# Moving the weight-staging loads of a recurrent block from SyncE's DMA queue to ScalarE's

## The chip, the cores and the metric

One Trainium2 chip. The program runs on 8 cores; each core takes one of the 8 sequences (4096 tokens of 1024 channels), and the cores exchange nothing. The metric is the device time of the slowest core, in microseconds, median of several runs.

## The reference, cut to what matters

```
xn = layernorm(x)                                  # no gain
h  = layernorm(xn) * gamma + beta
u, z = split(h @ in_proj_w, 2)                     # 1024 -> 2 x 2048
u  = silu(causal_conv4(u) + conv_b)
Bm = (u @ x_proj_w)[..., 16:]                      # 16 states
delta = softplus(u @ dt_proj_w + dt_proj_b)        # 2048 x 2048
h_t = h_{t-1} * exp(delta_t * A) + (u_t * delta_t) * Bm_t ;  y_t = sum over states
s  = ((y + u * D) * silu(z)) @ out_proj_w + xn
g  = silu(tanh(((xn @ weight) @ aux_weight1) @ aux_weight2 + bias))
out = x + s * g
```

The weights come as float32 in device memory; all matrix products run in bfloat16, so every weight is converted on the chip.

## The kernel before

The program is written as a list of instructions for each engine. A small recorder (class `Em`) keeps, for every buffer key, who wrote and who read it last, and puts the semaphore waits in. Each engine runs its own list strictly in the order in which the Python code emits it, and a DMA is an entry in the list of the engine that issues it: SP (SyncE) has nothing but DMAs, ACT (ScalarE) has activations and DMAs mixed. A DMA with its waits holds back everything behind it on its engine. All DMAs are recorded at line 102 or 108, so they are told apart by the tensors they move.

There are four stages, with a fence (all engines wait for all) between them:

- A start, where constants and the whole input projection `w_in` (16 pieces of 1 MB) are brought in.
- Stage A, 8 chunks of 512 tokens. In each chunk four `x` tiles are loaded (SP, two buffers `xb`), normalized twice on DVE with small helper activations on ACT (lines 321 to 348; the first ACT one is L333), transposed by PE, and multiplied by `w_in` (PE L408, ACT evictions L417 and L422). Then ACT stores the chunk's `up_sp` (2 MB) and calls `drain_w0(5)`.
- Stage B, 8 chunks of 512 tokens. Convolution on DVE (L465 to L480) from one buffer `upv` that SP loads from `up_sp`, silu on ACT (L484), 16 broadcast stores `bmrep_sp` from ACT's queue, the product with `w_dt` (PE L514), softplus (ACT L528 and L531), stores `d_sp` and `w_sp`; `drain_w0(5)` at the end of each chunk.
- The scan over time (L590 to L634), and the last stage with the output projection and the three feed-forward products.

`drain_w0` is the routine in question. It works through a list of 72 conversion jobs: 16 of `w_in` (all before stage A), 16 of `w_dt`, 16 of `w_out`, 24 of the three feed-forward weights. 40 of them stand at the ends of the 8 chunks of stage A (16 `w_dt`, 16 `w_out`, 8 `w_f`), and 16 in stage B (5, 5, 5 and 1 at the ends of the first four chunks). A job loads a float32 piece (1 MB for `w_in` and `w_dt`, 512 KB for the others) into one of two staging buffers `wstg0/1`, ACT converts it (L277 straight into `win_sb`, L297 into `wcv0/1`), and for all but `w_in` ACT's queue stores the bfloat16 piece to a scratch tensor (`wf_dt`, `wf_out`, `wf_f`; 512 or 256 KB). All stores of one scratch tensor have one key, so each waits until the one before has landed. In the kernel before the loads are SP's, so SP can be up to two jobs ahead of ACT; what stands behind them on SP, the `x` loads of the next chunk in stage A and the `up_sp` load of the next chunk in stage B, waits until SP is through with the chunk's loads.

Of the kernel before, what the change touches and what calls it, by code (L numbers as in the profile page):

```python
# [139 lines left out]
def build_program():  # L140
# [36 lines left out]
    em = Em()  # L177

    from contextlib import ExitStack
    with ExitStack() as stack:  # L180
# [36 lines left out]
        wstg = [WB.a([128, 2048], F32) for _ in range(2)]  # L217
# [45 lines left out]
        def drain_w0(njobs):  # L263
            for _ in range(njobs):
                i = w0_state["i"]
                if i >= len(w0_jobs):
                    return
                w0_state["i"] = i + 1
                kind, k, hh, dst = w0_jobs[i]
                par = i % 2  # L270
                if kind == "win":
                    src = w_in[k * 128:(k + 1) * 128, hh * 2048:(hh + 1) * 2048]
                    em.dma("sync", wstg[par][:], src,
                           reads=[], writes=[f"wstg{par}"],
                           stream=f"wstg{par}")
                    em.emit("scalar", lambda h, k=k, hh=hh, par=par:
                            h.activation(  # L277
                                win_sb[:, k, hh * 2048:(hh + 1) * 2048],
                                wstg[par][:], AF.Copy),
                            reads=[f"wstg{par}"], writes=["win"])  # L280
                else:
                    if kind == "dt":
                        src = w_dt[k * 128:(k + 1) * 128, :]
                        ncol = 2048
                        dkey = "wfdt"
                    elif kind == "out":
                        src = w_out[k * 128:(k + 1) * 128, :]
                        ncol = 1024
                        dkey = "wfout"
                    else:  # L290
                        src = (w_f1, w_f2, w_f3)[int(kind[1])][
                            k * 128:(k + 1) * 128, :]
                        ncol = 1024
                        dkey = "wf" + kind
                    em.dma("sync", wstg[par][:, 0:ncol], src,
                           writes=[f"wstg{par}"], stream=f"wstg{par}")
                    em.emit("scalar", lambda h, p=par, n=ncol: h.activation(  # L297
                        wcv[p][:, 0:n], wstg[p][:, 0:n], AF.Copy),
                        reads=[f"wstg{par}"], writes=[f"wcv{par}"])
                    em.dma("scalar", dst[k * 128:(k + 1) * 128, :],  # L300
                           wcv[par][:, 0:ncol],
                           reads=[f"wcv{par}"], writes=[dkey],
                           stream=f"wsc{par}")

        drain_w0(16)

        WK.reset()
# [44 lines left out]
        for c in range(NC):  # L352
            t0 = c * TC
            for ti in range(4):
                par = ti % 2
# [47 lines left out]
            for jo in range(2 * NJ):  # L403
# [16 lines left out]
                else:  # L420
# [9 lines left out]
                   reads=[f"up{cp}.{j}" for j in range(NJ)],  # L430
                   writes=[f"upsp{c}"], stream=f"upsp{cp}")
            drain_w0(5)

        em.fence()
# [15 lines left out]
        for c in range(NC):  # L450
# [57 lines left out]
            for jo in range(NJ):  # L508
                bk = jo % 4
                jp = jo % 2  # L510
                def mmfn(h, jo=jo, bk=bk, uc=uc):
                    ins = None
                    for k in range(NJ):
# [32 lines left out]
                       reads=[f"wv{jp}"], writes=[f"wsp{c}.{jo}"],  # L546
                       stream=f"wsp{jp}")
            drain_w0(5)

        em.fence()  # L550
# [115 lines left out]
        for c in range(NC4):  # L666
# [25 lines left out]
            for st in range(3):  # L692
                wsb = wfs[st]
                src = (xnc, h1, h2)[st]
# [40 lines left out]
            for ti in range(4):  # L735
                par = ti % 2
# [123 lines left out]
```

How the kernel before makes its waits and increments, by code:

```python
    def run(self, eng, handle, smap):  # L105
        for waits, fn, sem, amt in self.ops[eng]:
            for s, v in waits:
                handle.wait_ge(smap[s], v)
            ins = fn(handle)
            if ins is not None:
                ins.then_inc(smap[sem], amt)
```

## Time and profile before

| | us |
|---|---|
| median of 3 runs (lowest, highest) | 8546.5 (8543.9, 8580.69) |
| the profiled execution, its own time | 8539.65 |
| its span on the slowest core (core 3) | 8538.1 |
| start up to the first product, 0 to 151 | 151 |
| stage A, 151 to 1291 (without its first normalization) | 1140 |
| stage B, 1291 to 3005 | 1714 |
| scan, 3005 to 7490 | 4485 |
| last stage, 7490 to 8538 | 1048 |
| busy over the span: PE, DVE, ACT, POOL | 2755.4, 5205.2, 1809.1, 3246.4 |

How to read it: a row of the timeline gives the start, the busy time, the engine, the line, the operation with output and input, and in brackets how long the engine was idle before it and what ended that. `ACTq` and `SPq` are the DMA-issuing instructions of ACT and SP; their time is that of issuing, not that of the transfer. "Landing" is from the issue to the last byte's semaphore.

### The profile page before, as it was taken

What the parts mean: (1) busy time and instruction counts of PE and PEld (TensorE: products, weight loads), DVE (VectorE), ACT (ScalarE), POOL (GpSimd) and SP (SyncE); (2) the same over time, 40 slices, a digit from 0 to 9 for tenths busy, and PEclk for the clock granted to TensorE, in tenths of its full rate; (3) what the DMA queues carried; (4) which work ended last, traced back from release to release, by engine and by line L of the source; (5) the groups of instructions that cost most, each with busy time, mean ns of one, the idle gap of its engine ahead of it and who ended that gap; (6) DMA issues with size and microseconds to landing.
All of it is one profiled execution on the core that took longest, in us unless ns stands there. A gap on an engine that the chain in (4) does not pass through costs nothing.

```text
span 8538.1 us, 37387 instructions; the slowest of 8 cores (8502.7 to 8538.1 us)
## 1 busy us (share of the span) xinstructions
PE 2755.4 (32%) x9728; PEld 1013.9 (12%) x9728; DVE 5205.2 (61%) x2734; ACT 1809.1 (21%) x1683; POOL 3246.4 (38%) x524
## 2 busy tenths in 40 slices
PE   3344351222344412222222222222222222247666
PEld 1122120111111100000000000000000000013233
DVE  2332422333444469898989898999999999910000
ACT  3222220111111122221222122222222222201111
POOL 0000000000000074444555443999999999900000
PEclk9667675666666655555555555555555555568888
DMA  3322124444433320000000001000000000023332
GB/s 120 123 79 93 68 79 87 76 76 83 65 65 65 57 86 15 30 15 30 15 30 15 30 15 64 20 30 15 30 22 22 27 18 30 3 79 101 109 94 83
DMA packets 368734, 461.20 MB, mean 54 GB/s; under 512 B 149904, under 2 KB 297744, under 8 KB 360208
## 3 DMA queue, kind: packets, MB, share of 16 engines
q1 hardware_dynamic: 222352, 280.51, 10.8%
q10 hardware_dynamic: 146176, 178.31, 9.8%
q8 instruction: 85, 1.39, 0.1%
q14 instruction: 121, 0.99, 0.0%
HBM read 280.48 MB, written 178.26 MB: 54 GB/s over the span
## 4 chain that ended last, share of the span: by engine, by line
DVE 38%; DMA 14%; PE 14%; issue 13%; POOL 10%; ACT 6%; ACTq 4%; SPq 1%; DVEq 1%; POOLq 0%
DVE work L603 28%; POOL work L594 9%; PE psf L408 5%; PE psf L702 4%; ACTq L102 4%; DMA work<-wf_out 4%; DMA bmrep_sp<-bsb 2%; DMA d_sp<-work 2%; PE psf L683 1%; DVE work L470 1%; DVE work L480 1%; DVE work L475 1%; ACT work L531 1%; ACT work L484 1%; DVE work L534 1%
## 5 line engine op out<-in xcount | busy, mean ns | idle before, releaser
L594 POOL TENSOR_TENSOR work<-work,wrega 128x2048 bf16<-128x2048 bf16 x512 | 3182.9, 6237 | 4289.5 <-issue 3042.5
L616 PE MATMUL psf<-work,idb 128*128 128x512 bf16 x2048 | 955.1, 620 | 3487.5 <-DVE hstt L609 1752.1
L603 DVE TENSOR_TENSOR_SCAN work<-wregb,hstt,work 128x2048 bf16<-128x2048 f32 x128 | 1038.2, 8149 | 0.0
L603 DVE TENSOR_TENSOR_SCAN work<-work 128x2048 bf16<-128x2048 f32 x128 | 972.3, 7596 | 97.2 <-ACT wregb L590 45.8
L603 DVE TENSOR_TENSOR_SCAN work<-wregb,work 128x2048 bf16<-128x2048 f32 x128 | 1023.7, 7998 | 11.7 <-issue 0.9
L590 ACT ACTIVATE work<-work,aneg 128x2048 f32<-128x2048 f32 x256 | 508.5, 1998 | 2248.3 <-DVE work L634 1270.3
L603 DVE TENSOR_TENSOR_SCAN work<-work,hstt 128x2048 bf16<-128x2048 f32 x128 | 933.5, 7332 | 46.3 <-ACT work L590 41.5
L590 ACT ACTIVATE wregb<-work,aneg 128x2048 f32<-128x2048 f32 x256 | 508.5, 1998 | 1203.2 <-DVE work L603 1189.7
L616 PEld LDWEIGHTS psf<-work,idb 128*128 128x128 bf16 x2048 | 221.7, 126 | 4219.2 <-issue 4219.2
L514 PE MATMUL psf<-work,wrega 128*128 128x512 bf16 x2048 | 515.1, 413 | 430.7 <-DVE work L522 428.0
L534 DVE TENSOR_TENSOR work<-work 128x512 f32<-128x512 f32 x128 | 88.6, 692 | 701.9 <-ACT work L531 701.9
L321 DVE TENSOR_TENSOR work<-work 128x1024 f32<-128x1024 f32 x64 | 78.1, 1220 | 668.9 <-DMA work<-x_tm 665.5
L408 PE MATMUL psf<-work,wrega 128*128 128x512 bf16 x2048 | 467.6, 393 | 0.0
L728 POOL TENSOR_TENSOR wregb<-work 128x4096 f32<-128x4096 bf16 x8 | 63.3, 7907 | 984.3 <-ACT work L723 984.3
L749 DVE TENSOR_TENSOR work<-psf,work 128x1024 f32<-128x1024 f32 x32 | 39.2, 1224 | 521.3 <-PE psf L741 510.2
L702 PE MATMUL psf<-work,wrega 128*128 128x512 bf16 x1536 | 335.5, 379 | 15.7 <-ACT work L713 15.1
L683 PE MATMUL psf<-work 128*128 128x512 bf16 x1024 | 254.1, 408 | 235.8 <-DMA work<-wf_out 229.6
L689 DVE TENSOR_TENSOR work<-psf,work 128x512 bf16<-128x512 f32 x64 | 44.3, 691 | 436.0 <-PE psf L683 436.0
L514 PEld LDWEIGHTS psf<-work,wrega 128*128 128x128 bf16 x2048 | 206.5, 104 | 738.7 <-issue 620.2
L493 PE MATMUL psf<-work,xp 128*16 128x512 bf16 x128 | 46.4, 543 | 726.0 <-ACT work L484 582.4
L713 ACT ACTIVATE work<-psf 128x512 bf16<-128x512 f32 x128 | 76.4, 597 | 822.3 <-PE psf L702 822.3
L367 PE MATMUL psb<-idb,work 128*128 128x128 bf16 x256 | 32.4, 306 | 657.1 <-DVE work L348 657.1
(60 smaller groups left out, 2474.1 us busy)
## 6 DMA issues: line engine op xcount, KB each, us to landing
work<-x_tm SPq DMA_DIRECT2D x64, 512.0 KB, 5.3
d_sp<-work ACTq DMA_DIRECT2D x128, 256.0 KB, 2.1
work<-d_sp SPq DMA_DIRECT2D x32, 1024.0 KB, 4.8
work<-wf_out SPq DMA_DIRECT2D x64, 512.0 KB, 4.3
wregb<-w_in SPq DMA_DIRECT2D x16, 1024.0 KB, 6.0
wregb<-w_dt SPq DMA_DIRECT2D x16, 1024.0 KB, 7.8
sz_sp<-work ACTq DMA_DIRECT2D x128, 128.0 KB, 1.7
up_sp<-work ACTq DMA_DIRECT2D x8, 2048.0 KB, 11.5
```

Of the source, the lines that this page charges most:

```text
L102: return self.emit(eng, lambda h: h.dma_start(out=out_ap, in_=in_ap), reads=reads, writes=writes, dma=True, stream=stream)
L408: ins = h.matmul(bankf(bk), win_sb[:, k, jo * 128:(jo + 1) * 128], xh_fm[cp][:, k, :], start=(k == 0), stop=(k == NK - 1))
L470: h.scalar_tensor_tensor(a1[:], upv[:, j, 1:1 + TC], cwt3[:, 1, j:j + 1], a0[:], ALU.mult, ALU.add),
L475: h.scalar_tensor_tensor(a0[:], upv[:, j, 2:2 + TC], cwt3[:, 2, j:j + 1], a1[:], ALU.mult, ALU.add),
L514: ins = h.matmul(bankf(bk), wdt_sb[:, k, jo * 128:(jo + 1) * 128], uc[:, k, :], start=(k == 0), stop=(k == NJ - 1))
L534: em.emit("vector", lambda h, jp=jp: h.tensor_tensor(dout[jp][:], dpre[jp][:], dl[jp][:], ALU.max), reads=[f"dpre{jp}", f"dl{jp}"], writes ...
L590: h.activation(dab[sp][:], dj[jp][:], AF.Exp, scale=aneg3[:, j, s:s + 1]),
L594: h.tensor_tensor(pbf[sp][:], wj[jp][:], brep[:, s, :], ALU.mult),
L603: h.tensor_tensor_scan(hb[hp][:], dab[sp][:], pbf[sp][:], init, ALU.mult, ALU.add),
L616: ins = h.matmul(bankf(q), idb[:], hb[hp][:, q * 512:(q + 1) * 512], start=(s == 0), stop=False)
L683: ins = h.matmul(bankf(bk, TC4), wot[wp][:, k, :], ybc[:, k, :], start=(k == 0), stop=(k == NJ - 1))
L702: ins = h.matmul(bankf(bk, TC4), wsb[:, k, jo * 128:(jo + 1) * 128], src[:, k, :], start=(k == 0), stop=(k == NK - 1))
```

## The change

Both loads in `drain_w0` are issued from ACT's list instead of SP's. Sources, sizes, buffers, semaphores and the place in the Python code are as before.

```
                 if kind == "win":
                     src = w_in[k * 128:(k + 1) * 128, hh * 2048:(hh + 1) * 2048]
-                    em.dma("sync", wstg[par][:], src,
+                    em.dma("scalar", wstg[par][:], src,
                            reads=[], writes=[f"wstg{par}"],
                            stream=f"wstg{par}")
...
-                    em.dma("sync", wstg[par][:, 0:ncol], src,
+                    em.dma("scalar", wstg[par][:, 0:ncol], src,
                            writes=[f"wstg{par}"], stream=f"wstg{par}")
```

On ACT, at the start of the program, the row before (`wregb` is the staging and conversion memory, `wrega` holds `win_sb`):

```order
L242 ACTIVATE ddg<-wregb 128x2048
L246 ACTIVATE xp<-wregb 128x256
L277 ACTIVATE wrega<-wregb 128x2048 x16
L333 ACTIVATE cells<-cells 128x1
L339 ACTIVATE cells<-cells 128x1
```

and the same place now:

```order
L242 ACTIVATE ddg<-wregb 128x2048
L246 ACTIVATE xp<-wregb 128x256
L102 DMA wregb<-w_in 128x2048
L277 ACTIVATE wrega<-wregb 128x2048
L102 DMA wregb<-w_in 128x2048
L277 ACTIVATE wrega<-wregb 128x2048
L102 DMA wregb<-w_in 128x2048
L277 ACTIVATE wrega<-wregb 128x2048
```

Each of the 16 loads now stands behind the conversion of the load before it, and not in a list of its own.

On ACT, at the end of the first chunk of stage A (a piece of the difference; `up_sp` is the chunk's 2 MB store):

```order
 L102 DMA sz_sp<-work 128x512
 L102 DMA up_sp<-work 2048x1x512
+L102 DMA wregb<-w_dt 128x2048
 L297 ACTIVATE wregb<-wregb 128x2048
 L102 DMA wf_dt<-wregb 128x2048
+L102 DMA wregb<-w_dt 128x2048
 L297 ACTIVATE wregb<-wregb 128x2048
 L102 DMA wf_dt<-wregb 128x2048
+L102 DMA wregb<-w_dt 128x2048
 L297 ACTIVATE wregb<-wregb 128x2048
 L102 DMA wf_dt<-wregb 128x2048
```

Load, conversion and store of a job now stand one behind the other on one engine; the first load stands behind the `up_sp` store.

On SP, the row before, from the last constant on:

```order
L102 DMA wregb<-xpw_t 128x256
L102 DMA wregb<-w_in 128x2048 x16
L102 DMA work<-x_tm 128x1024 x4
L102 DMA wregb<-w_dt 128x2048 x5
L102 DMA work<-x_tm 128x1024 x4
L102 DMA wregb<-w_dt 128x2048 x5
```

and now:

```order
L102 DMA wregb<-xpw_t 128x256
L102 DMA work<-x_tm 128x1024 x32
L102 DMA wrega<-wf_dt 128x2048 x16
L102 DMA work<-up_sp 128x16x512
L102 DMA work<-up_sp 128x16x515 x7
```

Nothing stands between the `x` loads any more, nor between the `up_sp` loads. The lists of PE, DVE and POOL are unchanged.

## Rows read from the trace of the kernel before

**Rows 1.** Waits of DVE: engine, line, releaser: total us, times, longest.
```profile
DVE work L321 <- DMA work<-x_tm: 665.5, 8, 90.3
```
**Rows 2.** Windows, core 3: stretch, length, busy per engine, PEclk, DMA share, GB/s.
```profile
151.00:1291.00 1140.00, 523.24 (x2503) 249.71 (x2500) 321.49 (x617) 302.00 (x508) 0.00 (x0) 0.70 0.25 87
217.00:230.00 13.00, 0.00 (x0) 0.00 (x0) 0.00 (x0) 0.28 (x2) 0.00 (x0) 0.50 0.87 279
```
**Rows 3.** Timeline of ACT, start of the program: start, busy us, [idle before].
```profile
23.01 1.91 ACT L277 ACTIVATE wrega<-wregb 128x2048 bf16<-128x2048 f32 x1 [8.02 <-DMA wregb<-w_in]
...
88.35 0.20 ACT L333 ACTIVATE cells<-cells 128x1 f32<-128x1 f32 x1 [3.04 <-DVE cells L330]
```
**Rows 4.** Chain of waits, 60 to 90: start us, length us, what.
```profile
60.01 1.92 ACT wrega L277
...
62.00 5.67 DMA wregb<-w_in
...
67.81 1.92 ACT wrega L277
```
**Rows 5.** Timeline of ACT, end of stage A's first chunk.
```profile
212.27 0.56 ACTq L102 DMA_DIRECT2D up_sp<-work  x1
...
244.73 0.20 ACT L333 ACTIVATE cells<-cells 128x1 f32<-128x1 f32 x1 [1.41 <-DVE cells L330]
```
**Rows 6.** Timeline of SP in the same stretch.
```profile
214.92 17.39 SPq L102 DMA_DIRECT2D wregb<-w_dt  x3
232.35 16.54 SPq L102 DMA_DIRECT2D work<-x_tm  x3
```
**Rows 7.** Timeline of ACT, end of the fourth chunk.
```profile
680.33 0.54 ACTq L102 DMA_DIRECT2D up_sp<-work  x1
...
704.64 0.20 ACT L333 ACTIVATE cells<-cells 128x1 f32<-128x1 f32 x1 [3.81 <-DVE cells L330]
```
**Rows 8.** Timeline of ACT, end of the fifth chunk.
```profile
826.95 0.54 ACTq L102 DMA_DIRECT2D up_sp<-work  x1
...
850.47 0.20 ACT L333 ACTIVATE cells<-cells 128x1 f32<-128x1 f32 x1 [1.88 <-DVE cells L330]
```
**Rows 9.** Timeline of DVE behind stage A's last chunk (its up_sp: 1268.46).
```profile
1290.85 0.10 DVE L455 MEMSET work<- 128x48 bf16 x1 [81.41 <-DMA wf_f<-wregb]
```
**Rows 10.** Timeline of ACT, end of stage B's first chunk.
```profile
1550.05 0.33 ACTq L102 DMA_DIRECT2D w_sp<-work  x1
1550.75 1.06 ACT L297 ACTIVATE wregb<-wregb 128x1024 bf16<-128x1024 f32 x1 [2.57 <-DVE work L541]
...
1574.39 1.28 ACT L484 ACT_TABLE_LOAD   x1 [4.33 <-DVE work L480]
```
**Rows 11.** Timeline of DVE in the same stretch.
```profile
1571.26 0.49 DVE L465 TENSOR_SCALAR work<-work,cwt 128x512 f32<-128x512 bf16 x1 [21.35 <-DMA work<-up_sp]
```
**Rows 12.** Timeline of ACT, end of stage B's fourth chunk.
```profile
2208.92 0.33 ACTq L102 DMA_DIRECT2D w_sp<-work  x1
...
2212.16 1.28 ACT L484 ACT_TABLE_LOAD   x1 [1.76 <-DVE work L480]
```
**Rows 13.** Landing times of the w_dt loads (16).
```profile
DMA to landing us min/median/max: 5.7/7.8/11.7
```
**Rows 14.** Landing times of the w_out tensor's loads (16).
```profile
DMA to landing us min/median/max: 3.7/5.3/8.4
```
**Rows 15.** DMA issues between 1409 and 1424: KB, median us to landing.
```profile
u_sp<-work ACTq DMA_DIRECT2D x1, 2048.0 KB, 7.2
```
**Rows 16.** Landing times of wf_dt stores and reloads.
```profile
DMA to landing us min/median/max: 2.6/3.2/14.6
```
**Rows 17.** ACT behind the broadcast stores: first chunk of stage B.
```profile
1474.58 1.28 ACT L528 ACT_TABLE_LOAD   x1 [65.48 <-DMA bmrep_sp<-bsb]
```
**Rows 18.** The same in the fifth chunk, whose up_sp load runs beside it.
```profile
2333.30 1.28 ACT L528 ACT_TABLE_LOAD   x1 [68.22 <-DMA bmrep_sp<-bsb]
```

**Rows 19.** DMA issues of the whole program: KB each, median us to landing.
```profile
up_sp<-work ACTq DMA_DIRECT2D x8, 2048.0 KB, 11.5
```

More of the change, by code:

```diff
@@ L272, in drain_w0 @@
                     src = w_in[k * 128:(k + 1) * 128, hh * 2048:(hh + 1) * 2048]
-                    em.dma("sync", wstg[par][:], src,
+                    em.dma("scalar", wstg[par][:], src,
                            reads=[], writes=[f"wstg{par}"],
@@ L294, in drain_w0 @@
                         dkey = "wf" + kind
-                    em.dma("sync", wstg[par][:, 0:ncol], src,
+                    em.dma("scalar", wstg[par][:, 0:ncol], src,
                            writes=[f"wstg{par}"], stream=f"wstg{par}")
```

## The prediction

> **What bounds the kernel now.** I read the windows by stage first, then the waits of DVE, then the timelines of ACT, SP and DVE at each place where `drain_w0` stands. The scan and the last stage hold no job of `drain_w0` (it has 72: 16 at the start, 40 in stage A, 16 in stage B), so only the first 3005 us can move. In stage A PE is busy 523 of 1140 us and every other engine less [rows 2]: the chunks are a serial chain (normalize, multiply, convert weights, normalize), and DVE stands idle 665.5 us, 8 times, until an `x` load lands [rows 1]. That wait is mostly the product's time, but its last part is the weight jobs: SP holds the `x` loads back behind the third to fifth weight load of the chunk [rows 6]. So the stretch from the `up_sp` store to the next chunk's first helper activation L333 is exposed from end to end, in each chunk, and what happens to this stretch is the whole question. Its lengths now: first chunk 212.27 to 244.73 = 32.5 us [rows 5]; the next two, read the same way, 31.7 each; the fourth (one 1 MB job, four of 512 KB) 24.3 [rows 7]; the fifth 23.5 [rows 8], the sixth and seventh 23.1 and 24.0; the eighth, to the fence, 1268.46 to 1290.85 = 22.4 [rows 9].
>
> **What the change takes away and adds.** On SP nothing stands before the `x` and `up_sp` loads any more; they come a chunk ahead, under the product. On ACT a load now stands behind the conversion of the job before. An ACT instruction that waits for a DMA holds all behind it (ACT idles 65 us behind its own 16 broadcast stores [rows 17]), so two loads are never in flight: load, convert, store-issue, load. The two staging buffers are worth nothing. The work beside which loads ran (SP's prefetch of two jobs under the product of stage A, and the other buffer's conversion) no longer covers them.
>
> **One job in series.** `w_in`: a conversion ends, the next load issues and lands 5.67 us later, and the conversion of 1.91 us starts; the chain of waits shows just this loop for one buffer, 60.01 to 67.81 = 7.8 us [rows 4]. For `w_dt` the conversion is followed by the store's issue and then the load's (0.5 us together), the load alone takes 5.7 (the minimum of [rows 13]), I add 0.9 because the 512 KB store is just ahead of it in the same queue, 0.1 for the wake-up, and 1.91: 9.1 us. For the 512 KB jobs: 0.5 + 3.7 (the minimum of [rows 14]) + 0.5 + 0.1 + 1.06 [rows 10] = 5.9 us. The minima, not the medians, because the medians are of loads that overlapped with others, and now each is alone.
>
> **Start.** The first load lands at about 20.8 (15.06 + 5.7) and the 16th conversion ends at 20.8 + 15 x 7.8 + 1.9 = 139.7. L333 follows at once, since DVE's first four operations of chunk 0 have run by then; it is at 88.35 now [rows 3]. That is +51.4 us. The gain of the early `x` load (3.0 us of L333's wait) is in it.
>
> **Stage A.** First load of a chunk: it stands in ACT's queue behind the 2 MB `up_sp` store. A store of that size alone lands after 7.2 us [rows 15]; the load's data follow (2.6 us per MB at the 400 GB/s or so that this store and the quiet loads reach, 1.3 for 512 KB). So from the `up_sp` issue: 1 MB lands at 9.8, converted at 11.8; 512 KB at 8.5, converted at 9.7. Four more jobs and 0.45 us to L333: three `w_dt` chunks 11.8 + 4 x 9.1 + 0.45 = 48.7; the fourth 11.8 + 4 x 5.9 + 0.45 = 35.9; the fifth to seventh 9.7 + 23.6 + 0.45 = 33.7; the eighth 9.7 + 23.6 + 2.2 for the last store's landing = 35.5. Against the lengths above: +16.2, +17.0, +17.0, +11.6, +10.2, +10.6, +9.7, +13.1, in sum +105.4. The vanished `x` wait is counted: L333 follows the last job in mine, and waited for DVE in the old one.
>
> **Stage B.** From the last `w_sp` issue to the table load ahead of L484 it is 24.3 us now [rows 10], and it is the `up_sp` load that ends it: DVE waits 21.35 us for it [rows 11]. That wait goes, since SP now loads `upv` as soon as the convolution has read it. What is late next is ACT: 0.4 + 3.9 + 0.1 + 1.06 = 5.5 for the first job, 4 x 5.9, 0.4: 29.5 us. Against 24.3, 25.1 and 24.5 in the three chunks that is +14.6. The fourth chunk has one job: 5.9 against 3.2 [rows 12], +2.7. The prefetched `up_sp` load now runs beside the broadcast stores in the first three chunks also, as it already does from the fourth on, and there ACT's wait is 68.2 instead of 65.5 [rows 17, 18]: 3 x 2.8 = +8.4. Stage B: +25.7.
>
> **Sum.** 51.4 + 105.4 + 25.7 = +182.5 us on the profiled execution's 8539.65 gives 8722; the median of the runs is 7 above that execution, so 8728 us.
>
> **A rule against the trace.** The slowest `wf_dt` store, the first behind an `up_sp` store, takes 14.6 us to land, against 2.6 for the quickest [rows 16]: it stands behind the 2 MB in its queue while SP's loads run beside. The moved loads inherit this place. The Trainium skill (DMA: Bandwidth & Descriptors, section "Issuing engines are not separate DMA queues") says that transfers issued by any engine run on the same 16 DMA engines, so that choosing another issuer saves only issue time. By that rule alone the bytes need what they needed and the time would be unchanged; the trace agrees on the shared engines, but the rule says nothing of the order in which ACT comes to its own DMAs.
>
> The same page's "Anatomy of one DMA" prices a transfer at about 2.0 us and its bytes at 436 GB/s, an estimate of 4.4 us for a 1 MB load; by it the start would cost some +31 us instead of +51. It is given for another issuing path; the shortest `w_in` landing in the chain shown here is 5.67, and the sum goes by that.
>
> **Bounds.** Low: no penalty behind a store and slightly quicker lone loads (7.6, 8.2, 5.4 us a job), no contention in stage B: start +48, stage A +85, stage B +11, so +144, 8690. High: the first `w_in` load took about 7.9 us before its conversion [rows 3], so 10 us a job: +87; a load behind a store waits for its whole 2.6 us [rows 16] and `up_sp` takes the 11.5 us that it takes now in company [rows 19]: 10.8 and 7.4 us a job, first conversion at 16.1 or 14: stage A +191; stage B +54. Sum +332, 8879.
>
> **The rivals.**
> - Series and crowding (about 8870, the high sum). Eight cores draw on the memory at once, and if lone loads stay as slow as overlapped ones, the high case holds. For it: medians of 6 to 8 us per MB. Against it: the minima, and that the mean demand falls by almost half when each core pauses to convert.
> - No change (8545). The transfers, not their order, bound the stretch: the DMA engines are busy 0.87 of the time between 217 and 230 [rows 2], and the chunk's bytes are the same. Against it: the first chunk's 4.2 MB of later loads and stores plus the 2 MB need some 25 us even at full rate, but in series each job adds about 3 us of empty latency and 1.91 us of conversion in which nothing moves; and at the start there is no store at all to share with, yet a conversion and a latency come bare 16 times.
> - Faster (about 8500). ACT's issue could run ahead of an activation that waits, so that loads stay two ahead; then freeing SP is all gain. In 7 chunks L333 no longer waits for DVE (1.4, 3.8 and 1.9 us [rows 5, 7, 8], say 2), and the two `x` loads no longer fall among the jobs (1 MB, 2.6 us): 7 x 4.6 = 32. The start gains 3 [rows 3], and three chunks of stage B the 4.3 us that ACT idles there [rows 10], 13: 48 in all. The point from which it decides is a 1 MB job at or below its present pace, about 6 us (32.5 for five, [rows 5]). Against it: ACT's 65 us of idleness behind its own issues [rows 17].
>
> **How the numbers follow.** Series as summed 0.84, crowding 0.11, no change 0.03, faster 0.02. A measurement tells about 0.5% (43 us) from no change. The first two are slower by more than that: 0.95; no change 0.03; faster 0.02. The range for 8 in 10 is 8665 to 8810: below the low sum by a little, since lone loads may be quicker than any row shows, and up into the crowded case.
>
> **What would show it.** In the changed profile: 16 conversions L277 about 7.8 us apart, and L333 first at about 140; from an `up_sp` issue in stage A to L333 about 49 us in the first chunks and 34 in the fifth; DVE's long wait at L321 gone, and one for ACT at L336 in its place; no DVE wait for `up_sp` from stage B's second chunk on, but one for ACT at L470; scan and last stage as before. Conversions 4 us apart would prove the series wrong, and jobs of 10 us the size of it.

## The result and the profile after

The changed kernel takes 8685.57 us (median of 10 runs, 8657.53 to 8761.15) against 8547.33 (10 runs, 8525.96 to 8580.69): a ratio of 1.0156, 95% interval 1.0134 to 1.0178, or about +138 us between the medians. The ratios here and below leave out executions in which the cores of one die ran at a lower granted clock and took over 1% longer than the other's. The forecast was 8728 with a range of 8665 to 8810, so the sign and the place were right and the size was a third too large. The profiled execution's slowest core is core 5, with a span of 8680.8.

Cores differ by some 40 us in one execution, so I compare stages by the median over the eight cores of each profile. The marks are the first L333, the memset L455 behind the fence, and the first exponential of the scan, L590; each column is a mark minus the one before.

| us | to L333 | stage A | stage B | scan to end | span |
|---|---|---|---|---|---|
| before | 85.2 | 1197.7 | 1741.8 | 5489.9 | 8516.2 |
| after | 102.2 | 1302.0 | 1759.8 | 5488.4 | 8655.5 |
| difference | +17.0 | +104.3 | +18.0 | -1.5 | +139.3 |
| forecast | +51.4 | +105.4 | +25.7 | 0 | +182.5 |

The start, as the timeline of ACT on core 5 of the changed kernel has it (start us, busy us, engine, line, operation, idle before); it answers to [rows 3, 4]:

```profile
22.96 1.91 ACT L277 ACTIVATE wrega<-wregb 128x2048 bf16<-128x2048 f32 x1 [7.35 <-DMA wregb<-w_in]
22.98 0.34 ACTq L102 DMA_DIRECT2D wregb<-w_in  x1
28.52 1.91 ACT L277 ACTIVATE wrega<-wregb 128x2048 bf16<-128x2048 f32 x1 [3.65 <-DMA wregb<-w_in]
28.54 0.34 ACTq L102 DMA_DIRECT2D wregb<-w_in  x1
...
101.25 1.91 ACT L277 ACTIVATE wrega<-wregb 128x2048 bf16<-128x2048 f32 x1 [3.29 <-DMA wregb<-w_in]
103.07 0.19 ACT L333 ACTIVATE cells<-cells 128x1 f32<-128x1 f32 x1
```

The next load is issued 0.02 us after the conversion in front of it has begun, not after it has ended at 24.87. Conversions are about 5.2 us apart, which is one load. The chain of waits (start, length, what) says the same with no conversion in it; in [rows 4] the conversions stood in the chain:

```profile
59.95 5.03 DMA wregb<-w_in
...
65.14 4.99 DMA wregb<-w_in
...
70.28 4.99 DMA wregb<-w_in
```

The end of stage A's first chunk on the same core, which answers to [rows 5]:

```profile
225.83 0.56 ACTq L102 DMA_DIRECT2D up_sp<-work  x1
226.41 2.24 ACTq L102 DMA_DIRECT2D wregb<-w_dt  x1
240.02 1.91 ACT L297 ACTIVATE wregb<-wregb 128x2048 bf16<-128x2048 f32 x1 [14.63 <-DMA wregb<-w_dt]
242.00 0.33 ACTq L102 DMA_DIRECT2D wf_dt<-wregb  x1
242.36 0.45 ACTq L102 DMA_DIRECT2D wregb<-w_dt  x1
249.84 1.91 ACT L297 ACTIVATE wregb<-wregb 128x2048 bf16<-128x2048 f32 x1 [7.91 <-DMA wregb<-w_dt]
...
275.93 1.91 ACT L297 ACTIVATE wregb<-wregb 128x2048 bf16<-128x2048 f32 x1 [6.55 <-DMA wregb<-w_dt]
277.97 0.33 ACTq L102 DMA_DIRECT2D wf_dt<-wregb  x1
278.40 0.20 ACT L333 ACTIVATE cells<-cells 128x1 f32<-128x1 f32 x1 [0.56 <-ACT wregb L297]
```

Here the series is real: the store waits for the conversion's end (240.02 + 1.91, issued at 242.00), the load stands behind the store, and the jobs are 8.5 to 9.8 us apart. Core 3, the core of the rows of before, shows from the `up_sp` issue to L333 49.1, 49.0, 47.9, 37.4, 33.1, 32.9 and 33.2 us, and 35.2 to the fence, against 32.5, 31.7, 31.7, 24.3, 23.5, 23.1, 24.0 and 22.4 before: +104.6.

The waits of DVE on core 5 (engine, line, releaser: total us, times, longest); the first and the last answer to [rows 1], the second to [rows 11]:

```profile
DVE cells L336 <- ACT cells L333: 806.7, 64, 109.8
...
DVE work L470 <- ACT work L484: 121.9, 119, 25.3
...
DVE work L321 <- DMA work<-x_tm: 10.9, 1, 10.9
```

The 665.5 us at L321 are down to 10.9, in the first chunk alone. The wait has moved on to L336, the first DVE operation that needs ACT, and grown (on core 3, where the 665.5 were, it is 781.0, after 28.3 before). In stage B the 21.35 us for `up_sp` have become 25 us for ACT. In both stages the transfer that was late is now early, and DVE waits longer.

### The profile page after: what moved, and what is told of

It reads as the page before. It is cut to its first block, busy times and chain, and to the rows that moved or that the text cites. A ratio compares the mean times of both kernels' runs of the same rounds, so it can differ in the third digit from the quotient of the medians.

```text
span 8680.8 us, 37320 instructions; the slowest of 8 cores (8636.7 to 8680.8 us)
## 1 busy us (share of the span) xinstructions
PE 2735.9 (32%) x9728; PEld 1011.1 (12%) x9728; DVE 5204.0 (60%) x2734; ACT 1810.0 (21%) x1683; POOL 3245.8 (37%) x524
## 4 chain that ended last, share of the span: by engine, by line
DVE 37%; DMA 16%; PE 13%; issue 13%; POOL 10%; ACT 6%; ACTq 4%; SPq 1%; DVEq 1%; POOLq 0%
DVE work L603 27%; POOL work L594 9%; PE psf L408 6%; PE psf L702 4%; DMA work<-wf_out 3%; ACTq L102 3%; DMA bmrep_sp<-bsb 3%; DMA d_sp<-work 2%; DMA wregb<-w_dt 1%; DVE work L480 1%; DVE work L470 1%; DVE work L475 1%; ACT work L531 1%; ACT work L484 1%; DMA wregb<-w_f 1%
## 5 line engine op out<-in xcount | busy, mean ns | idle before, releaser
L590 ACT ACTIVATE work<-work,aneg 128x2048 f32<-128x2048 f32 x256 | 508.7, 1999 | 2246.0 <-DVE work L634 1268.8
L590 ACT ACTIVATE wregb<-work,aneg 128x2048 f32<-128x2048 f32 x256 | 508.7, 1999 | 1202.5 <-DVE work L603 1189.0
L336 DVE SCALAR_TENSOR_TENSOR cells<-cells 128x1 f32<-128x1 f32 x64 | 10.2, 159 | 806.7 <-ACT cells L333 806.7
L702 PE MATMUL psf<-work,wrega 128*128 128x512 bf16 x1536 | 335.5, 379 | 15.7 <-ACT work L713 15.1
```

Source lines behind the costliest of these rows:

```text
L590: h.activation(dab[sp][:], dj[jp][:], AF.Exp, scale=aneg3[:, j, s:s + 1]),
L702: ins = h.matmul(bankf(bk, TC4), wsb[:, k, jo * 128:(jo + 1) * 128], src[:, k, :], start=(k == 0), stop=(k == NK - 1))
```

## The experiments

Theory 1 was formed from the timeline above: a load issue on ACT is not held by the conversion that is still running in front of it, since it needs nothing of it; what holds it is an instruction in between that does need it, the store. Theory 2 is the prediction's: load, conversion, load strictly in series. Each expectation below says what its own theories 1 and 2 are. The stages of all runs are medians over the eight cores of each profile, in us. The column "0.61" is steadier than the ratio: over all executions it takes the dies whose four cores had a median granted clock of 0.61 or more, and gives their median span less that of such dies of the kernel before, run beside it (2 to 14 dies a run, 12 to 32 of before; no interval). The changed kernel's own such dies take 8648.3.

| | to L333 | stage A | stage B | scan to end | ratio to before, 95% interval | 0.61 |
|---|---|---|---|---|---|---|
| only w_in | 102.8 | 1226.4 | 1742.9 | 5487.6 | 1.0039 (1.0000 to 1.0078) | +14 |
| only the rest | 85.2 | 1297.4 | 1762.5 | 5482.8 | 1.0160 (1.0093 to 1.0227) | +121 |
| one w_in buffer | 130.8 | 1321.1 | 1759.8 | 5494.5 | 1.0246 (1.0189 to 1.0303) | +167 |
| stores on SP | 102.7 | 1276.7 | 1742.5 | 5489.4 | 1.0070 (1.0030 to 1.0110) | +63 |
| two ahead on ACT | 85.2 | 1175.7 | 1719.5 | 5490.3 | 0.9946 (0.9908 to 0.9984) | -50 |
| loads on GpSimd | 87.6 | 1218.4 | 1732.2 | 5492.1 | 0.9984 (0.9950 to 1.0018) | -10 |
| x first on SP | 86.9 | 1183.2 | 1729.0 | 5492.2 | 0.9951 (0.9922 to 0.9981) | -26 |
| spread, GpSimd | 88.7 | 1043.4 | 1703.0 | 5497.1 | 0.9786 (0.9733 to 0.9838) | -188 |
| spread, ACT | 82.8 | 1043.9 | 1708.3 | 5490.2 | 0.9773 (0.9720 to 0.9826) | -191 |

**Only the loads of w_in moved.**

```
# kernel before, the "win" branch alone
-                    em.dma("sync", wstg[par][:], src,
+                    em.dma("scalar", wstg[par][:], src,
```

> Only the 16 loads of w_in are issued from ACT, the other 56 stay on SP. Theory 1 (a load issue on ACT does not wait for the conversion in front of it, since it needs nothing of it; only the landing of the load itself is exposed): conversions L277 are about 5.2 us apart, the first L333 comes at about 103 us instead of 86, and the time is 15 us above the kernel before, about 8562. Theory 2 (load, conversion, load strictly in series, as I predicted): conversions 7.8 apart, L333 at 140, +51, about 8600.

Measured: 8609.29 us (10 runs, against 8583.02 of before beside it), ratio 1.0039. Conversions 5.2 us apart, first L333 at 103.6 on core 5. The start is theory 1's to within a microsecond. The total, expected at +15, is blurred by the granted clock: stage A, which has no edit here, takes 1195.8 us on its best core and 1226.4 in the median, so the evidence is the first column and the +14 of the dies at 0.61.

**Only the other 56 loads moved.**

```
# kernel before, the other branch alone
-                    em.dma("sync", wstg[par][:, 0:ncol], src,
+                    em.dma("scalar", wstg[par][:, 0:ncol], src,
```

> Only the other 56 loads are issued from ACT, those of w_in stay on SP. Both theories: the ends of stage A's chunks take 49, 49, 48, 37, 33, 33, 33 us from the up_sp issue to L333 as with the whole change, stage B's three about 26.6, and the time is 110 to 125 us above the kernel before, about 8665; with the run of the w_in loads alone it should add up to the whole change's +138. If a large part of the whole change's loss lay in a slower PE and not in the jobs, this run would lie under +100.

Measured: 8698.64 us, ratio 1.0160; stage A +99.7 and stage B +20.7 over before, the start unchanged. With the 17.6 us that the start of the run above takes longer this adds up to the whole change's +138, and the loss lies in the jobs. (The dies at 0.61 add up to +135. The two ratios add up to 1.0199, more than 1.0156, but within their intervals.) Core 5's chunk ends take 49.3, 49.2, 49.3, 37.5, 33.6, 33.5 and 37.1 us.

**One staging buffer for w_in.**

```
# changed kernel
-                par = i % 2
+                par = 0 if kind == "win" else i % 2
```

> The whole change, and the w_in jobs use one staging buffer instead of two, so that each load has to wait for the conversion before it. Theory 1: conversions L277 go from 5.2 to about 7.1 us apart (5.1 + 1.9 + 0.1), the first L333 to about 132 us, the time 27 to 30 us above the changed kernel. Theory 2 (the loads are already in series and the start is short for another reason, quick lone loads): nothing changes, 5.2 apart and L333 at 103.

Measured: L333 at 130.8 instead of 102.2, +28.6; time 8778.65, ratio 1.0246. The timeline of ACT on core 5:

```profile
31.20 1.91 ACT L277 ACTIVATE wrega<-wregb 128x2048 bf16<-128x2048 f32 x1 [6.17 <-DMA wregb<-w_in]
33.18 0.33 ACTq L102 DMA_DIRECT2D wregb<-w_in  x1
38.35 1.91 ACT L277 ACTIVATE wrega<-wregb 128x2048 bf16<-128x2048 f32 x1 [5.24 <-DMA wregb<-w_in]
```

Now the load is issued at 33.18, when the conversion has ended at 33.11. The one difference is the dependence through the buffer, so it is the dependence and not the place in the list that put the conversion into the loop. This is the series that I had predicted for the change, and it takes about 7.1 us a job. The total moved more than the start, +93 against the changed kernel's median. On one die of the profile the clocks are 0.594 to 0.597, and stage A, which the edit doesn't touch, is 19 us longer in the median. The dies at 0.61 take 8679.2 against the changed kernel's 8648.3, +31, which is the start's, where 27 to 30 were expected.

**The stores moved to SP.**

```
# changed kernel; besides, SP's next two x loads and next up_sp load are put ahead of the jobs
-                    em.dma("scalar", dst[k * 128:(k + 1) * 128, :],
+                    em.dma("sync", dst[k * 128:(k + 1) * 128, :],
```

> The whole change, and the stores of the converted weights are issued from SP instead of ACT; so that they don't hold back SP's other loads, the next chunk's first two x loads and the next up_sp load of stage B are put ahead of the jobs on SP. ACT's list holds only loads and conversions. Theory 1 (it is the store, which must wait for the conversion, that keeps the next load back): 1 MB conversions L297 come 5.8 us apart instead of 8.4 and 512 KB ones about 4.1 instead of 5.4; up_sp to L333 about 38, 38, 37, 31, 28, 28, 28 us; the time is about 75 us under the changed kernel, 8610. Theory 2 (strict series): conversions 7.7 and 4.9 apart, about 25 us under it.

Measured: 8633.92 us, ratio 1.0070. That is 52 below the changed kernel's median, but the kernel before that was run beside it took 8583.02 and not 8547.33; by the ratios, 1.0156 less 1.0070, it is 74, and the dies at 0.61 say 73, where 75 were expected. Core 5, first chunk:

```profile
253.06 1.91 ACT L297 ACTIVATE wregb<-wregb 128x2048 bf16<-128x2048 f32 x1 [3.50 <-DMA wregb<-w_dt]
253.13 0.34 ACTq L102 DMA_DIRECT2D wregb<-w_dt  x1
258.43 1.91 ACT L297 ACTIVATE wregb<-wregb 128x2048 bf16<-128x2048 f32 x1 [3.45 <-DMA wregb<-w_dt]
258.50 0.33 ACTq L102 DMA_DIRECT2D wregb<-w_dt  x1
```

Without the store between them the `w_dt` load too starts beside the conversion, and the jobs are mostly 5.4 us apart instead of 8.5 to 9.8. The chunk ends are 37.7, 40.2, 38.8, 30.6, 27.7, 28.3 and 28.0 us, as theory 1 had them. In sum these seven are 54 us shorter than the changed kernel's on core 5; the stage's median gained only 25 in a profile with clocks of 0.598 to 0.608.

**All loads on ACT, two jobs ahead.** Two loads stand before the first job, and one behind each job.

```
# changed kernel; load_w0() issues the next load of the list into the buffer just freed
+        load_w0()
+        load_w0()
...
                     em.dma("scalar", dst[k * 128:(k + 1) * 128, :], ...
+                load_w0()
```

> All loads on ACT as in the changed kernel, but written two jobs ahead: behind each conversion (and its store) stands the load for the job after the next, into the buffer just freed, and at a chunk's end the next chunk's first two jobs are already loaded. Theory 1 (what costs is the place of the load behind the job before it in an in-order list, not the queue it is on): the cost goes and the freed SP remains: L333 at about 83 us, up_sp to L333 about 30 us in the first three chunks and 20 to 22 from the fourth on, stage B's three ends below 20, the time about 8515, under the kernel before. Theory 2 (ACT's queue as such is the worse place, its loads lie behind the 2 MB store and cost it issue time): the ends stay above 40 and 28 us and the time above 8600.

Measured: 8533.27 us (9 runs, 8482.19 to 8620.85), ratio 0.9946; the median span of its profile is 8468.2, 48 below the kernel before's. On core 5 the first chunk's end takes 28.7 us and the fifth's 20.2:

```profile
205.24 0.55 ACTq L102 DMA_DIRECT2D up_sp<-work  x1
205.89 1.91 ACT L306 ACTIVATE wregb<-wregb 128x2048 bf16<-128x2048 f32 x1 [1.09 <-issue]
207.88 0.33 ACTq L102 DMA_DIRECT2D wf_dt<-wregb  x1
...
218.35 0.33 ACTq L102 DMA_DIRECT2D wf_dt<-wregb  x1
...
233.92 0.20 ACT L343 ACTIVATE cells<-cells 128x1 f32<-128x1 f32 x1 [1.04 <-issue]
```

The queue is the changed kernel's; only where the loads stand in ACT's list differs, and the loss of 138 us is a gain of 50 on the dies at 0.61. Stage B's first three ends, expected below 20, take 13.8 to 14.4. Theory 2 of this run (ACT's queue is itself the worse place) falls.

**The loads on GpSimd.**

```
# kernel before, in both branches
-                    em.dma("sync", ...
+                    em.dma("gpsimd", ...
```

> The kernel before with the two loads of drain_w0 issued from GpSimd, which does nothing else up to the scan. No load stands behind a conversion in a list, and none holds back SP. Theory 1: L333 at about 83 us, the ends of stage A's chunks about 30 and 21 us, stage B's 20, the time about 8510. If freeing SP gained nothing (a rival for why the change lost: that the freed loads only compete), it would be the kernel before, 8545.

Measured: 8550.37 us, ratio 0.9984 with 1 inside the interval: no gain to be told, where 35 us were expected; the dies at 0.61 gain 10, where they spread over 32 us. The start is 2.4 us later than before, and stage B 9.6 shorter. Stage A is 1186.6 on the best core, 8 below that of before, but 1218.4 in the median. The expectation that failed is that of the chunk ends. They were to take about 30 and 21 us; over the eight cores their medians are 33.7, 34.0, 32.9, 24.3, 23.8, 23.2, 21.5 and 23.3. A core's eight ends sum to 216.0 us in the median, against 217.2 in the kernel before and 195.1 in the run two ahead on ACT. So theory 1's words for this run, that nothing is held back once no load stands behind a conversion, are too simple. Core 5, first chunk, shows the wait that stayed:

```profile
212.08 0.33 ACTq L102 DMA_DIRECT2D wf_dt<-wregb  x1
...
228.72 0.33 ACTq L102 DMA_DIRECT2D wf_dt<-wregb  x1
229.15 1.91 ACT L297 ACTIVATE wregb<-wregb 128x2048 bf16<-128x2048 f32 x1 [14.73 <-DMA wf_dt<-wregb]
```

ACT waits for the first store, which was issued behind the 2 MB `up_sp` store, and two loads of GpSimd's queue run beside it. The kernel before has the same wait at the same place (core 3, in the stretch of [rows 5]), so its chunk ends are not bounded by loads alone:

```profile
230.00 1.91 ACT L297 ACTIVATE wregb<-wregb 128x2048 bf16<-128x2048 f32 x1 [12.72 <-DMA wf_dt<-wregb]
```

From the first to the second store of the first three chunks it takes 14.5, 14.9 and 15.7 us here (medians over the cores), 15.7, 14.5 and 13.9 before, and 11.3, 9.9 and 9.6 in the run two ahead on ACT. The rest of stage A's median, some 20 us, goes with this profile's mean clocks of 0.601 to 0.609; whether they had to do with the edit I can't say.

**The loads on SP, but x and up_sp first.**

```
# kernel before; the two x loads of chunk c + 1 are emitted here, and in stage B its up_sp load
+            if c + 1 < NC:
+                for ti in range(2):
+                    em.dma("sync", xb[ti][:], x_tm[...next rows...], ...)
             drain_w0(5)
```

> The kernel before, loads on SP, but SP issues the next chunk's first two x loads and the next up_sp load of stage B ahead of the jobs' loads. It gives the gain of freed SP alone, without any loss on ACT: L333 follows the last conversion by 0.5 us instead of 1.4 to 3.8, the ends of stage A's chunks about 2 us shorter than before, those of stage B about 20 instead of 24.5, less 3 us each for the up_sp load beside the broadcast stores; the time 20 to 30 us below the kernel before, about 8520. The changed kernel had this gain in it, so its gross loss is about 160.

Measured: 8519.4 us, ratio 0.9951; stage A -14.5, stage B -12.8. This is what SP's freedom is worth by itself, 27 us (26 on the dies at 0.61), and it is in the changed kernel's net: with it the gross loss is about 165. The first store of its first chunk stands against two `w_dt` loads of SP's queue, and the next store, which waits until it has landed, comes 16.1 us later (core 5, 212.90 and 228.97):

```profile
212.90 0.36 ACTq L102 DMA_DIRECT2D wf_dt<-wregb  x1
...
228.97 0.33 ACTq L102 DMA_DIRECT2D wf_dt<-wregb  x1
```

In the run with everything on ACT, two jobs ahead, the same stretch takes 10.5 us (207.88 to 218.35). There a single load stands behind the store, in the same queue. Over the cores the medians of the first three chunks are 16.1, 15.2 and 15.0 against 11.3, 9.9 and 9.6. That this makes that version the better by 7.5 us in stage A is read from the traces; no run separates the queue from the number of loads beside the store.

**The jobs spread through the chunks**, with the loads on GpSimd and then on ACT two ahead.

```
# at the end of the body of stage A's product loop, and so in stage B's loop over jo
-            drain_w0(5)
+                if jo % 6 == 5:        # stage B: if jo % 3 == 2
+                    drain_w0(1)
```

> Loads from GpSimd, and the five jobs of a chunk are no longer at its end but spread through it: one behind every sixth eviction of stage A's product, one behind every third iteration of stage B's. The conversions of 1.9 us fit between evictions 1.7 us apart with four banks in hand. If the whole cost of the jobs is that they stand exposed at the chunk ends, L333 follows the up_sp issue within 2 us, stage A loses about 200 us and stage B about 60: 8285. If the transfers or ACT slow the product down as much as they free, the time stays at 8500.

> The jobs spread through the chunks as in the run with GpSimd's loads, but the loads issued from ACT two jobs ahead. Theory 1 (place in the list decides, the queue does not): the same as with GpSimd's loads or a little better, first L333 at 84 to 86, stage A about 1042 us, stage B about 1700, and a time near 8330 on undisturbed cores, 2.5% below the kernel before. Theory 2 (ACT's queue is itself a handicap): stage A 20 us or more longer than with GpSimd's loads.

Measured: 8399.74 us, ratio 0.9786, and 8409.00 us, ratio 0.9773 (before beside it 8592.47). Stage A 1043.4 and 1043.9, stage B 1703.0 and 1708.3. The first was expected at 8285, which took the whole of the exposed ends for gain; 154 of the 200 us in stage A came, and 39 of 60 in stage B. ACT of the second, core 0, in the product of the first chunk:

```profile
158.28 0.60 ACT L427 ACTIVATE work<-psf 128x512 bf16<-128x512 f32 x1 [1.13 <-PE psf L418]
158.77 1.90 ACT L306 ACTIVATE wregb<-wregb 128x2048 bf16<-128x2048 f32 x1
160.75 0.34 ACTq L102 DMA_DIRECT2D wf_dt<-wregb  x1
161.11 0.46 ACTq L102 DMA_DIRECT2D wregb<-w_dt  x1
161.67 1.09 ACT L427 ACTIVATE work<-psf 128x512 bf16<-128x512 f32 x2 [1.00 <-PE psf L418]
...
189.69 0.60 ACT L432 ACTIVATE work<-psf 128x512 bf16<-128x512 f32 x1 [4.16 <-DMA sz_sp<-work]
...
203.68 0.60 ACT L432 ACTIVATE work<-psf 128x512 bf16<-128x512 f32 x1 [4.42 <-DMA sz_sp<-work]
```

In the first half the conversion fits between evictions. In the second half ACT waits up to 4.4 us for a 128 KB `sz_sp` store, which now lands among the weight transfers, since the eviction writes into one of only two small buffers. That some of the missing 46 us lie there is read from the trace, not tested. The two queues give the same stage A to 0.5 us, and the same total to 3 us on the dies at 0.61: with the jobs spread and the load well ahead, the issuing engine does not matter. With the jobs at the chunk ends the two runs that load two ahead differ, -10 us from GpSimd against -50 from ACT; which part of that is the queue, and which the moment at which the loads go out, is open. The rule of the Trainium skill that the prediction weighed (DMA: Bandwidth & Descriptors, "Issuing engines are not separate DMA queues") agrees with the spread runs. It says nothing of where in its engine's list a load stands.

## Why the prediction was right or wrong

**The forecast as a whole.** The sign, the stages and the size within the range came true, in part by luck. The measured 8686 lies 4 us under the prediction's own low sum of 8690; it is inside the range because the lower edge was set below that sum. What happened, some jobs in series and others not, was none of the rivals. The signs that the prediction named for its mechanism, conversions 7.8 us apart and L333 at about 140, did not appear at the start.

**Exposed ends, and the engine that sets them: right.** All of the loss lies ahead of the scan (-1.5 us behind it), in the 72 jobs. The freed `x` and `up_sp` loads did come early, and DVE's waits went where the prediction sent them, to L336 and L470.

**One job in series: wrong for w_in, right for the jobs with a store.** The step that failed is "a conversion ends, the next load issues", 7.8 us a job and +51.4 for the start; measured 5.2 and +17.0. I took the loop of [rows 4], in which a load waits for the conversion of its own buffer, for the loop of the changed kernel, in which it goes into the other buffer and waits for nothing that still runs. The 65 us of ACT's idleness behind its broadcast stores [rows 17] show that ACT runs its list in order; they don't show that an issue waits for an activation still running. The run with one buffer brings the predicted loop about, at 7.1 us a job. A lone load is also quicker than any row of before, 4.99 us against 5.67, and that accounts for about 0.7 us a job of the 2.6.

For the `w_dt` jobs the series needed no such assumption, since the store really waits: 9.1 forecast, 8.25 measured on core 3 (conversions start 13.6 and, four jobs on, 46.6 us after the first `up_sp` issue); for the 512 KB jobs 5.9 against 5.4 (9.9 to 31.5 in the fifth chunk).

**Stage A: +105.4 against +104.3, with two errors that cancel.** The first conversion of a `w_dt` chunk was put at 9.9 us after the `up_sp` issue and starts at 13.6, 12.8 and 12.1 on core 3 (14.2 on core 5, 240.02 less 225.83): 2 to 4 us too early, against 3.4 us too much in the four jobs that follow. The term that was too small is the 7.2 us of the 2 MB store, taken from `u_sp` [rows 15]; the `up_sp` store takes 11.1 (core 3, first chunk: KB, us to landing), and the load lands some 2.5 us behind it, near the 2.6 forecast. Why the two stores of one size differ no run shows.

```profile
up_sp<-work ACTq DMA_DIRECT2D x1, 2048.0 KB, 11.1
```

In the 512 KB chunks the first conversion was forecast 1.3 to 1.6 us too early (8.6 against 9.9 to 10.2) and the four jobs behind it 2 us too long; their ends were forecast at 33.7 and take 32.9 to 33.2.

**Stage B: +25.7 against +18.0.** The end of a chunk was put at 29.5 us and is 26.6 to 26.7: the five jobs again, about 0.5 us too long each. The cost of the prefetched `up_sp` load beside the broadcast stores was put at 2.8 us a chunk; core 3 shows 67.6, 67.5 and 67.3 from the `u_sp` issue to L528, where 65.4, 65.0 and 65.1 stood, 2.3 each. In the fourth chunk 70.7 became 68.2, a gain that was not forecast.

**The rivals.** Crowding (8870; its own sum says 8879) did not come: lone loads are quicker, not slower, so the medians of overlapped loads were the wrong price, as argued. No change is excluded by the interval. Its bytes were also misread: 8.67 MB move in the first chunk's 32.5 us, not 4.2 and 2, and the 6.2 that were written would need 16 us and not 25 at the 400 GB/s named. Of the faster one, the mechanism was half right: ACT's issue does run past an activation in front of it, only not past one that an instruction between them waits for. Where the loads are written ahead, its gain appears, at a ratio of 0.9946.

**Sum.** The error of 44 us is 34 in the start, 8 in stage B, 1 in stage A and the 1.5 behind them. The start's term was a quarter of the sum and rested on a reading of a loop in a kernel with another order.

## What to carry to other kernels

A DMA moved onto an engine that computes takes that engine's list for its clock: look at the instruction just ahead of it, and ask whether that one waits for something. A load ahead of which stands a store of the result just computed can't be prefetched, however many buffers there are; the same load on the same queue written two jobs earlier turned +1.6% into -0.5%. Work that stands alone at the end of a chunk is worth more moved under the chunk's product (-2.2%) than the choice of its queue.

## What the runs showed of the hardware

- A DMA issue on ACT starts while an activation in front of it runs: 22.98 beside 22.96, for an activation of 1.91 us. With a wait on that activation it comes 0.07 us behind its end (33.18 against 33.11).
- One 1 MB load by itself lands in 4.9 us at best and 5.1 in the median (16 loads, all cores loading at the same time), where two in flight took 6.0 each and 4.0 a job (core 3 of the kernel before, conversions from 23.0 to 83.4).
- A load issued just behind a 2 MB store on the same queue held ACT for 2.24 us at its issue (226.41), against 0.45 for the next ones.
- Behind a 512 KB store that stood behind a 2 MB store, the next could be issued after 10.5 us with one load behind it in the same queue, and after 16.1 and 16.6 with two loads in another queue (core 5, first chunk: loads on SP, on GpSimd).
- A 2 MB store landed in 7.2 us as `u_sp` [rows 15], and in 10.6 to 11.7 over the eight cores as `up_sp` with a load behind it.
- The product of a stage A chunk took 56.2 to 57.8 us on five cores of the changed kernel. On core 5 the first took 58.3 at a granted clock of 0.97, and the fifth 65.75 at 0.83. While TensorE is idle at the chunk ends its clock is near the lower level, 1.2 GHz (0.51 between 226 and 278). Such differences between cores are as large as several of the effects here, and are why stages were compared by medians over the cores.
